# Graph attention on one core: the selection matrix is made from two tensor operands (places and a broadcast lane number) in place of a tensor and a per-partition scalar

## What is computed

```python
q = (x @ Wq + bq).reshape(n, H, C); k = (x @ Wk + bk)...; v = (x @ Wv + bv)...
e = (ea @ We).reshape(-1, H, C)
alpha = jnp.einsum('ehc,ehc->eh', q[dst], k[src] + e) / jnp.sqrt(jnp.float32(C))
amax = jax.ops.segment_max(alpha, dst, num_segments=n)
ex = jnp.exp(alpha - amax[dst])
w = ex / (jax.ops.segment_sum(ex, dst, num_segments=n)[dst] + 1e-16)
out = jax.ops.segment_sum((v[src] + e) * w[:, :, None], dst, num_segments=n).reshape(n, D)
return out + x @ Ws + bs
```

## Time and profile before

| | |
|---|---|
| median of 3 runs | 3104.43 us (3102.76 to 3106.22) |
| profiled execution | 3110.81 us, its span 3108.8 us |
| busy in the span | PE 2081.9 us, PEld 1701.2, DVE 1982.6, ACT 1180.9, POOL 1929.2 |
| POOL's gathers, first to last start | 695.3 to 2974.9 us |
| mean granted clock of TensorE | 0.685 |

### The profile page before, as it was taken

One profiled execution on the slowest core, in us unless ns is written; L12 is line 12 of the kernel. 1 busy time (PEld: TensorE's weight loads), 2 busy tenths in 40 slices (PEclk: granted clock), 3 DMA queues, 4 the chain that ended last, 5 costly groups with the idle time before them and its releaser, 6 DMA issues. The chain is left out here.

```text
span 3108.8 us, 65603 instructions
## 1 busy us (share of the span) xinstructions
PE 2081.9 (67%) x14712; PEld 1701.2 (55%) x14713; DVE 1982.6 (64%) x5172; ACT 1180.9 (38%) x3628; POOL 1929.2 (62%) x2138
## 2 busy tenths in 40 slices
PE   4556899984676676667667565566666766666650
PEld 3434799973555555555555443455555555555540
DVE  5555222234777777777777575577777777777757
ACT  1000355541444444444444342244444444444444
POOL 3600122227777777777777547777777777777726
PEclk6665899995666666666666587566667666666655
DMA  7789311114444444444444613444444444444442
GB/s 209 225 254 270 106 37 37 37 51 138 132 126 132 131 132 130 132 132 124 131 129 128 71 38 126 126 131 132 132 132 131 127 129 131 127 131 132 114 36 83
DMA packets 274898, 384.86 MB, mean 124 GB/s; under 512 B 120652, under 2 KB 206620, under 8 KB 274524
## 3 DMA queue, kind: packets, MB, share of 16 engines
q0 software_dynamic: 80768, 220.05, 25.8%
q1 hardware_dynamic: 144476, 163.04, 16.7%
q10 hardware_dynamic: 49536, 0.55, 0.9%
HBM read 360.42 MB, written 23.02 MB: 123 GB/s over the span
## 5 line engine op out<-in xcount | busy, mean ns | idle before, releaser
L1353 POOL DMA_INDIRECT wide<-kv,a_source x1664 | 1630.3, 980 | 512.8 <-issue 474.2
L1388 PE MATMUL psum<-wide,a_hot 128*128 128x136 f32 x3328 | 751.7, 392 | 145.0 <-DVE acc L1588 144.5
L1377 PE MATMUL psum<-wide,a_hot_t 128*128 x4992 | 642.7, 282 | 272.9 <-DVE a_product L1505 244.2
L1388 PEld LDWEIGHTS psum<-wide,a_hot 128*128 128x128 f32 x3328 | 639.7, 277 | 195.2 <-DVE acc L1588 119.2
L1377 PEld LDWEIGHTS psum<-wide,a_hot_t 128*128 128x128 bf16 x4992 | 516.3, 118 | 407.4 <-issue 328.6
L1588 DVE TENSOR_TENSOR acc<-acc,psum 128x136 f32 x1664 | 488.0, 293 | 256.7 <-issue 51.5
L1454 ACT ACTIVATE a_hot<-iota_n,a_spot 128x128 f32<-128x128 f32 x1664 | 526.6, 390 | 37.8 <-PE psum L1388 37.8
L1505 DVE TENSOR_TENSOR a_product<-psum,wide 128x512 f32<-128x512 f32 x416 | 286.9, 690 | 385.7 <-DMA wide<-kv,a_source 245.4
L1446 ACT ACTIVATE a_edge_q<-psum 128x16 f32<-128x16 f32 x416 | 76.6, 184 | 1140.0 <-PE psum L1388 1027.7
L1458 ACT ACTIVATE a_hot<-a_hot,ones 128x512 f32<-128x512 f32 x416 | 300.3, 722 | 13.5
L1508 DVE TENSOR_REDUCE a_score<-a_product 128x16 f32<-128x512 f32 x416 | 286.1, 688 | 14.2
(11 more groups left out here) (265 smaller groups left out, 2183.3 us busy)
## 6 DMA issues: line engine op xcount, KB each, us to landing
acc<-in_edge_attr SPq DMA_DIRECT2D x344, 192.0 KB, 3.6
a_place<-places SPq DMA_DIRECT2D x104, 512.0 KB, 3.8
wide<-kv,a_source POOLq DMA_INDIRECT x1664, 3.3
kv<-acc SPq DMA_DIRECT2D x49, 128.0 KB, 1.7
kv<-p_pairs SPq DMA_DIRECT2D x24, 256.0 KB
c_node<-drec ACTq DMA_DIRECT2D x344, 1.5 KB
a_cut<-breaks SPq DMA_DIRECT2D x208, 8.1 KB
acc<-in_x SPq DMA_DIRECT2D x49, 64.0 KB, 1.8
```

Source lines behind the costliest of these rows:

```text
L1353: pool.indirect_dma_start(out=ring[:, at.b, n, :], out_offset=None, in_=kv[:, :], in_offset=bass.IndirectOffsetOnAxis(ap=source[at.b][:, n ...
L1377: last = pe.matmul(query_out(q)[:, t, :], hot_t[:, b, q * QUAD + t, :], rows, start=(s == 0), stop=(s == SPLIT - 1), skip_group_check=True)
L1388: last = pe.matmul(sum_out(q, t), hot[q % 2][:, t, :], ring[:, (at.b + back) % 2, q * QUAD + t, LEAD:KV], start=True, stop=True, skip_grou ...
```

## The change

`make_hot` compares `place` with `lane` as a second tensor, read over and over with a step of 0 along 2048 columns, where it compared `place` with `lane` as a per-partition scalar. Nothing else is edited. On PE, ACT, POOL and SP the program's instructions and their order are the same; on DVE each `TENSOR_SCALAR` of L1497 has become a `TENSOR_TENSOR` at the same place, with the same waits.

```diff
             def make_hot(at, later, h):
                 at.wait(place_in[h], 16, 16 + 16 * later)
-                dve.tensor_scalar(hot_t[:, (at.b + later) % 2, h * HALF:(h + 1) * HALF, :].rearrange("p t e -> p (t e)"),
-                                  place[h][:, :], lane[:, 0:1], None, ALU.is_equal).then_inc(made_hot, 1)
+                dve.tensor_tensor(hot_t[:, (at.b + later) % 2, h * HALF:(h + 1) * HALF, :].rearrange("p t e -> p (t e)"),
+                                  place[h][:, :], repeat(lane[:, 0:1], 1, HALF * P), ALU.is_equal).then_inc(made_hot, 1)
```

## The result

| | before | after |
|---|---|---|
| median | 3105.32 us (4 runs) | 3263.51 us (4 runs, 3259.89 to 3266.45) |
| profiled execution | 3110.81 us, span 3108.8 | 3261.52 us, span 3258.8 |
| ratio | | 1.051 (95% interval 1.0497 to 1.0522) |

The changed kernel is 5.1% slower, 158 us.

A forecast was written before the change was run, and what follows sets the result against it. The prediction took POOL's back-to-back gathers as the bound: holds behind L1497 add 153 us in the loops and 5 ahead of them, 158 on 3104.4, so 3262 us, range 3222 to 3308.

The forecast's parts named there:

- POOL's gathers are the bound: In both attention stretches POOL issues gathers back to back, never waiting over 0.3 us; a microsecond added there lengthens the kernel.
- The instruction's length: L1497 as a two-tensor instruction over 2048 columns takes 2.28 us, in place of 0.746.
- two columns at a time: Rival: the bf16 operand lets L1497 take 1.22 us, so 48 us more, 3152 us; 4 in 100.
- It holds a gather as L1565 does: A gather starting within L1497 waits for its end, then needs 0.82 us; each hold grows by 1.53 us.
- The sum: Longer holds on POOL, 153 us in the loops and 5 ahead of them, add 158 us.
- In the loops: 100 of the 104 L1497 instructions each hold one gather 1.53 us longer: 153 us.
- the starts of the layers: Comparison pairs ahead of the loops hold nothing now, then one gather 2.7 us longer: 5 us in both layers.
- What was left out: L1565 in steps 5 and 7 shifts against POOL: at most 50 us more or 25 less, not in the sum.
- DVE's extra time is hidden: DVE's 160 us more in L1497 cost nothing by themselves, since DVE and PE have margin to POOL.
- no hold: Rival: the second operand does not collide with a gather's start; L1497's 27 us of holds go, 3077 us; 5 in 100.
- slower than one column a cycle: Rival: L1497 takes 4.4 us or 5.6, so 3474 us or more, or some 3600; 4 in 100.
- nothing changes: Rival: L1497 in a form as fast as the old one holds gathers about as long as now; 2 in 100.

The follow-up runs named there:

- experiment 5: The changed kernel with the lane number as one bf16 element with a step of 0: 3258.82 us, ratio 1.0501 to the kernel before.
- experiment 4: The changed kernel with the lane number as a row of 16 bf16 columns in SBUF, read 128 times over: 3166.63 us, ratio 1.0187 to the kernel before.
- experiment 2: The kernel before with an unused reduction of 1408 columns (one SBUF input) behind each selection matrix: 3120.79 us, ratio 1.0044.
- experiment 1: The changed kernel with the lane number, L1497's second operand, read from PSUM: 3099.14 us, ratio 0.9971 to the kernel before.
- experiment 6: The changed kernel with the comparison 0.58 us earlier in steps 4 and 6, ahead of the last two additions: 3274.44 us, ratio 1.0546 to the kernel before.
- experiment 3: The changed kernel with the comparison in four instructions of 512 columns: 3138.26 us, ratio 1.0092 to the kernel before.

## Why the prediction was right, step by step

- **POOL's gathers are the bound.** Right: the table above, and POOL's waits after, where no idle is over 0.3 us.
- **The instruction's length.** 2.28 us forecast from three two-tensor rows, 2.284 measured. That `lane` is float32 was not the whole of it: experiment 5 has a bf16 operand and takes 2.284 us. The 1.22 us that I set against "two columns at a time" were measured in experiment 4, 1.218.
- **It holds a gather as L1565 does.** Right, and this was the step with a rule against it. What the Trainium skill, "SBUF — State Buffer", "Who interferes with whom", infers from an earlier probe, that a two-tensor instruction leaves descriptor generation alone, differs from what stands here: a gather within L1497 takes 2.91 us where its second operand is in SBUF and 0.95 where it is in PSUM. The Trainium skill's other sentence there, that an instruction with two SBUF inputs collides with a GpSimd instruction that reads SBUF, agrees with both numbers: the gather reads its indices, `a_source`, from SBUF.
- **The sum.** I went through all 1664 gathers of both traces and put each one over 1.0 us down to the VectorE instruction behind whose end it finishes by some 0.82 us. In the loops L1497's holds go from 28 us (98 gathers) to 179 (100 gathers), 151 more; the term was 153. The held gathers start 0.34 us into the instruction in the mean before and 0.37 after: the forecast that they would start as far into it as before came true. At the starts of the layers the holds go from 4.7 to 9.9 us, where the term was 5. That agreement is luck, for I read the place wrongly: in the kernel before, the pair does hold a gather, one that the earlier trace rows do not show. It starts while `acc` is being cleared (L1631), 1.70 us ahead of the pair, and is held until the end of the first of the two comparisons. Before:

```profile
694.15 5.61 DVE L1631 MEMSET acc<- 128x6664 f32 x1 [3.43 <-issue]
...
697.98 3.15 POOL L1353 DMA_INDIRECT wide<-kv,a_source  x1 [0.30 <-issue]
```

After, where the next gather is held as well, through the second comparison:

```profile
693.63 5.61 DVE L1631 MEMSET acc<- 128x6664 f32 x1 [3.43 <-issue]
...
697.33 4.89 POOL L1353 DMA_INDIRECT wide<-kv,a_source  x1 [0.30 <-issue]
699.16 4.42 DVE L1497 TENSOR_TENSOR a_hot_t<-a_place,lane 128x2048 bf16<-128x2048 bf16 x2
...
702.52 1.88 POOL L1353 DMA_INDIRECT wide<-kv,a_source  x1 [0.31 <-issue]
```

The clearing alone does not hold it. In experiment 5 the comparisons ahead of the loop wait until `acc` is cleared, and a gather that starts as far into the clearing (3.67 us, against 3.70 after) is not held:

```profile
691.54 5.61 DVE L1633 MEMSET acc<- 128x6664 f32 x1 [1.33 <-issue]
...
695.21 0.96 POOL L1354 DMA_INDIRECT wide<-kv,a_source  x1 [0.30 <-issue]
696.47 0.95 POOL L1354 DMA_INDIRECT wide<-kv,a_source  x1 [0.30 <-issue]
697.19 4.49 DVE L1498 TENSOR_TENSOR a_hot_t<-a_place,a_lane_b 128x2048 bf16<-128x2048 bf16 x2
```

- **What was left out.** L1565's holds, by the same account, went from 14 to 10 us; I had bounded them at 25 down and 50 up. All gathers together are 152 us longer. With the forecast of 158 us and the 158 measured between the medians the agreement is closer than the terms deserve: the spans of the two profiled executions differ by 150.
- **DVE's extra time is hidden.** Right: experiment 2 pays 13 us for 167, and experiment 1 pays nothing for the same 829 us.

The rivals of the prediction: *no hold* is what the kernel does once the operand is in PSUM, and it was priced at 3077; the runs gave 3099 and 3073, since L1565's holds depend on the phase (39 and 13 us by the same account). *Two columns at a time* is what experiment 4 has; in the changed kernel it did not occur, nor did *slower than one column a cycle* or *nothing changes*.

## What to carry to other kernels

Look first for the engine that never waits; here it was GpSimd, issuing gathers back to back, and the price of a VectorE instruction was how long it made a gather wait, not how long it ran. An instruction on another engine can cost such a bound most of its length (in experiment 6 a hold of 2.05 us behind one of 2.29) while its own time is hidden. Here, moving its second operand to PSUM gave that back, and cutting it in four gave back 125 of 158 us. Before an operand is swapped for "the same thing broadcast", ask of its form twice: how many columns at a time it leaves, and which memory's reads it adds.

## What the runs showed of the hardware that was not expected

- A gather held by a VectorE instruction gets in between two that stand back to back (experiment 3: released at the first piece's end). But a comparison that stands behind a clearing of 128x6664 with no wait between holds a gather that started ahead of it, within the clearing (1.7 us ahead before, 1.8 after); with a wait between (experiment 5) it does not. How an instruction holds a gather ahead of its own start is open.
- A broadcast element costs the second column even where all operands are bf16 (2.284 us), a row of 16 columns read over and over does not (1.218 us in SBUF, 1.214 in PSUM).
- The phase between VectorE and GpSimd is worth some tens of us by itself: with the comparison moved by half a microsecond (experiment 6), L1565 held gathers for some 52 us in all, against 10 in the changed kernel with the same instructions.
